# A two-layer graph network kernel: five PE transpositions per step become DMA transpositions of split rows

## The reference

```
# layer 0, x and adj of one graph; 8 heads of 32, 4 edge types
q, k = x @ Wq + bq, x @ Wk + bk
attn = softmax(q k^T / sqrt(32))                     # per head
out  = sum over r of (attn * (adj == r)) @ (x @ Wv[r] + bv[r])
x1   = LN(x + out @ Wo + bo) * g1 + beta1
x2   = LN(x1 + gelu(x1 @ W1 + b1) @ W2 + b2) * g2 + beta2
# layer 1, 8 heads of 32
e    = leaky(q k^T, 0.2), masked by adj > 0          # q, k, v = x2 @ Wq, Wk, Wv
h    = softmax(e) @ v
out  = LN(concat(LN(h) * g1 + b1, x2) @ Wffn^T) * g2 + b2 + x2
```

## Time and profile before

| | us |
|---|---|
| median of 3 runs | 2527.88 (2527.27 to 2528.18) |
| the profiled execution | 2530.18 |
| its span, first to last instruction | 2528.3 |
| PE busy | 2430.5 (96%) |
| ACT busy | 2212.6 (88%) |
| DVE busy | 2122.6 (84%) |
| POOL busy | 1925.9 (76%) |

### The profile page before, as it was taken

The page is one execution under the profiler, slowest core; times in us unless marked ns, Lnnn a source line. Parts: engine busy times, 40 slices in busy tenths (PEclk is TensorE's granted clock), DMA queues, the critical chain, the costliest instruction groups (busy, mean ns, idle before and its releaser), DMA issues. The chain is left out here.

```text
span 2528.3 us, 83141 instructions
## 1 busy us (share of the span) xinstructions
PE 2430.5 (96%) x31496; PEld 1984.4 (78%) x31496; DVE 2122.6 (84%) x3730; ACT 2212.6 (88%) x6224; POOL 1925.9 (76%) x2126
## 2 busy tenths in 40 slices
PE   3899999999999999999999999999999999999984
PEld 2678888888888888888888888878888888888873
DVE  3788888888889888889888888888888888888863
ACT  4699999989989989989989989989989989999973
POOL 1477787787788778778778778778778778778774
PEclk9999999999999999999999999999999999999997
DMA  5234433533433433443442442442443443443332
GB/s 135 58 55 83 93 61 80 93 67 75 93 71 71 93 75 67 93 78 63 94 82 59 94 83 59 93 87 59 88 92 57 85 94 60 81 93 61 77 64 47
DMA packets 610636, 196.75 MB, mean 78 GB/s; under 512 B 539328, under 2 KB 609472, under 8 KB 610240
## 3 DMA queue, kind: packets, MB, share of 16 engines
q1 hardware_dynamic: 607072, 188.02, 38.5%
q10 hardware_dynamic: 3168, 3.41, 0.5%
HBM read 40.38 MB, written 16.78 MB: 23 GB/s over the span
## 5 line engine op out<-in xcount | busy, mean ns | idle before, releaser
L982 DVE TENSOR_TENSOR pm<-pT,bank 128x4096 f16<-128x4096 f16 x256 | 567.6, 2279 | 0.0
L459 PE MATMUL bank<-wv,xT 128*128 128x512 f16 (+1 forms) x2304 | 456.6, 344 | 0.0
L1172 POOL TENSOR_TENSOR h<-h_f,h 128x512 f16<-128x512 f32 x256 | 297.3, 1174 | 117.5 <-ACT h L730 117.5
L459 PE MATMUL bank<-yT,w 128*128 128x256 f16 x3072 | 356.8, 273 | 1.2 <-DVE yT L944 1.2
L754 ACT ACTIVATE bank<-bank,p_nmax 128x128 f32<-128x128 f32 x1024 | 353.9, 364 | 4.4 <-DVE p_nmax L968 4.3
L459 PE MATMUL bank<-w,h 128*128 128x256 f16 x3072 | 347.3, 273 | 2.8 <-POOL h L1172 2.8
L459 PEld LDWEIGHTS bank<-wv,xT 128*128 128x128 f16 x2304 | 225.2, 98 | 148.3 <-issue 0.5
L743 ACT ACTIVATE p<-p,p_nmax 128x128 f32<-128x128 f32 x1024 | 336.0, 437 | 1.3 <-DVE p_nmax L961 0.6
L459 PEld LDWEIGHTS bank<-yT,w 128*128 128x128 f16 x3072 | 295.1, 98 | 42.8 <-issue 1.6
L459 PEld LDWEIGHTS bank<-w,h 128*128 128x128 f16 x3072 | 296.5, 98 | 37.4 <-issue 2.9
L1172 POOL TENSOR_TENSOR p1h<-p,p1h 128x512 f16<-128x512 f32 x256 | 296.6, 1159 | 30.5 <-ACT p1h L784 30.4
(11 more groups left out here) (127 smaller groups left out, 5663.7 us busy)
## 6 DMA issues: line engine op xcount, KB each, us to landing
x_sb<-in_x_dram SPq DMA_DIRECT2D x64, 256.0 KB, 3.4
adj_i<-in_adj_dram SPq DMA_DIRECT2D x128, 128.0 KB, 2.8
out_dram<-x2b SPq DMA_DIRECT2D x64, 256.0 KB, 2.3
pT<-p0h SPq DMA_TRANSPOSE x128, 4.9
pT<-p1h SPq DMA_TRANSPOSE x128, 4.7
pm<-in_L_gnn_W_dram ACTq DMA_DIRECT2D x1, 1024.0 KB, 13.6
pm<-in_L_gnn_W_dram SPq DMA_DIRECT2D x1, 1024.0 KB, 16.9
h_f<-in_L_gnn_Wffn_dram SPq DMA_DIRECT2D x1, 512.0 KB, 10.3
```

The source lines that it names most:

```text
L459: last = nc.tensor.matmul(o, l, r, start=(first and k == 0), stop=(k == len(todo) - 1))
L982: V_.tensor_tensor(pm0[g][:, s], pT0[g][:, s].unsqueeze(1).broadcast_to([P, REL, HEADS, P]), edges[:, g].unsqueeze(2).broadcast_to([P, REL ...
L1172: return V_.tensor_tensor(to, source, high, ALU.subtract)
```

## The change

- The five arrays are split into halves while still rows: ACT copies the high half into `x_rows`, `o0_rows`, `x1_rows`, `x2_rows`, `o1_rows` and POOL subtracts for the low half. SP then issues one `DMA_TRANSPOSE` of 256 KB for each (`transpose_rows`, line 427 of the new kernel), and PE waits for its landing. The twenty PE transposes of a pair are gone, and so are DVE's four low halves.
- The norm factor of `o1` is multiplied into the first half of Wffn in the preamble, and its shift becomes a row `w_bias`, added by one matmul of 512 columns per pair. `attention_affine_1` is gone.
- The norms of x1, x2 and the output run on DVE, in PSUM: one `scalar_tensor_tensor` subtracts the mean and multiplies by the factor row, a second multiplies by the root and adds the shift row (for the output, x2b). POOL's six large operations and two small ones, and ACT's `last_rows_normed`, are gone.
- x has three buffers and not two, and the bias bo is added in place. All lists of jobs are in another order, and so is `PE_BANKS`. The pipeline has 7 extra steps instead of 8.

```diff
+    ("f", 2, 3, "x2_ready", 1, 1),
+    ("v0_0", 1, 1, "v0_lo", 4, 1),
...
+                def transpose_x(m):
+                    sp.wait_ge(S["xT0_lo"], m + 1)
+                    if past(m):
+                        sp.wait_ge(S["v0_ps"], 4 * m)
+                        sp.wait_ge(S["q0_ps"], m)
+                        sp.wait_ge(S["k0_ps"], m)
+                    transpose_rows(xT0, x_rows, S["xT0_in"])
...
                 def x_transposed(m):
-                    pe.wait_ge(S["xT0_lo"], m + 1)
+                    pe.wait_ge(S["xT0_in"], 16 * m + 16)
...
                 def last_product(m):
                     u = m % 2
                     bank_free("w", m)
-                    pe.wait_ge(S["oT1_lo"], m + 1)
+                    pe.wait_ge(S["oT1_in"], 16 * m + 16)
                     x2_transposed(m)
+                    nc.tensor.matmul(ps("w")[:], ones16[:], w_bias[:].unsqueeze(1).broadcast_to([P, G, D]), start=True, stop=False)
...
                 def x1_high(m):
-                    act.wait_ge(S["yT0_ps"], m + 1)
-                    if past(m):
-                        act.wait_ge(S["h_ps"], 4 * m)
-                    nc.scalar.activation(flat(yT0[:, 0]), ps("yT0")[:], copy).then_inc(S["yT0_hi"], 1)
+                    act.wait_ge(S["x1_ready"], m + 1)
+                    if past(m):
+                        act.wait_ge(S["yT0_in"], 16 * m)
+                    nc.scalar.activation(x1_rows[:, 0], by_chunk(x1[:]), copy).then_inc(S["yT0_hi"], 1)
...
+                def centred_gained(name, gain, m):
+
+                    mv = ln[name][1]
+                    dve.wait_ge(S[name + "_mean"], 2 * m + 2)
+                    for g in range(G):
+                        last = V_.scalar_tensor_tensor(rows_in(name, g), rows_in(name, g), mv[:, g, 0:1], gain[:],
+                                                       ALU.subtract, ALU.mult)
+                    last.then_inc(S[name + "_gained"], 1)
+
+                def scaled_added(name, to, added, m):
+
+                    rs = ln[name][3]
+                    dve.wait_ge(S[name + "_gained"], m + 1)
                     dve.wait_ge(S[name + "_rstd"], m + 1)
                     for g in range(G):
-                        V_.tensor_scalar(rows_in(name, g), rows_in(name, g), mv[:, g, 0:1], rs[:, g:g + 1], ALU.subtract,
-                                         ALU.mult).then_inc(S[name + "_normed"], 1)
+                        last = V_.scalar_tensor_tensor(to[:, g], rows_in(name, g), rs[:, g:g + 1], added(g), ALU.mult, ALU.add)
+                    return last
...
+                def x1_low(m):
+                    pool.wait_ge(S["yT0_hi"], m + 1)
+                    low(x1_rows[:, 1], by_chunk(x1[:]), x1_rows[:, 0]).then_inc(S["yT0_lo"], 1)
```

More of the change, by code:

```diff
@@ L140, in build @@
         ident16 = sb("ident16", [P], BF16)
-        minus_half, minus_one = (sb(n, [G]) for n in ("minus_half", "minus_one"))
-        x_sb = [sb(f"x_sb{u}", [G, D]) for u in range(2)]
-        xbo = [sb(f"xbo{u}", [G, D]) for u in range(2)]
+        minus_half = sb("minus_half", [G])
+        w_bias = sb("w_bias", [D], F16)
+        x_sb = [sb(f"x_sb{u}", [G, D]) for u in range(XR)]
         adj0_i = sb("adj0_i", [G, P], I32)
@@ L327, in _ @@
                     last.then_inc(s_ffnT, 1)
+                pe.wait_ge(s_fold, 3 * KC)
+                for c in range(KC):
+                    last = nc.tensor.matmul(bank[2 * KC][:, 0:D], b1_cols[:, c], unscaled[:, c], start=(c == 0), stop=(c == KC - 1))
+                last.then_inc(s_ffnT, 1)
         S = {name: ctx.enter_context(nc.semaphore(name)) for names in SEMAPHORES.values() for name in names}
@@ L362, in pipeline, with landed @@
                 steps(n)
-        def landed(m):
-            return 16 * (m // 2) + 16
+        def landed(m, buffers):
+            return 16 * (m // buffers) + 16
         def flat(t):
@@ L453, in bank_free, with products @@
                         pe.wait_ge(*bank_before(job, m))
-                def products(o, pairs, first=True):
+                def products(o, pairs, first=True, final=True):
                     todo = [(l[i], r[j]) for l, r in pairs for i, j in ((0, 0), (0, 1), (1, 0))]
                     for k, (l, r) in enumerate(todo):
-                        last = nc.tensor.matmul(o, l, r, start=(first and k == 0), stop=(k == len(todo) - 1))
+                        last = nc.tensor.matmul(o, l, r, start=(first and k == 0), stop=(final and k == len(todo) - 1))
                     return last
@@ L829, in probs_high_0, with attention_high_1 @@
                                          copy).then_inc(S["p0_hi"], 1)
-                def last_rows_normed(m):
-                    act.wait_ge(S["w_shift"], m + 1)
+                def attention_high_1(m):
+                    act.wait_ge(S["o1_normed"], 2 * m + 2)
                     if past(m):
-                        act.wait_ge(S["out_ready"], m)
-                    for g in range(G):
-                        last = nc.scalar.activation(w_n[:, g], ps("w")[:, g * D:(g + 1) * D], ACT.Identity,
-                                                    scale=ln["w"][3][:, g:g + 1], bias=w_shift[:, g:g + 1])
-                    last.then_inc(S["w_normed"], 1)
@@ L1160, in _ @@
+                    if live(n):
+                        probs_low_0(n, 0)
                 pipeline(steps)
```

755 lines of the change are left out of this document (355 added, 400 removed).

## The result

The changed kernel takes 2407.75 us, the median of four runs (2403.04 to 2410.49); the kernel before, beside it, 2528.03. The ratio is 0.9519, 95% interval [0.9507, 0.9532]: 120 us less. The forecast was 2427, its own range 2415 to 2445, rival A (no stalls) 2409, and the range with 8 in 10 was 2400 to 2490. So the time lies in the wide range, outside the forecast's own, and on A's number. The profiled execution took 2403.04 us, with a span of 2401.2.

The account below looks back on a forecast made before the run. PE was taken as the bound, 37.67 us a step: span 2528.3 - 122.7 (PE work) + 17.7 (waits) + 4.0 (fill) = 2427.3, then + 1.9 - 2.3 = 2427 us. Own range 2415 to 2445; 8 in 10, 2400 to 2490.

Parts of the forecast that it names:

- rival A: PE in the steady steps: no stall at all, the forecast without its 17.7 us of waits, 2409 us; chance 0.22.
- PE's floor 35.59: PE's work in a step: 37.67 less 2.30 for the transposes plus 0.22 for the new matmul, 35.59 us.
- six take 1.30, one 0.22: The added w_bias matmul on PE: six matmuls of 512 columns take 1230.79 to 1232.09, so one costs 0.22 us.
- Waits 0.3 a step: PE's waits for the new transpositions to land: 0.3 us a step, 17.7 us in all.
- small spares: Landing before PE needs the array: x 0.3 us ahead, x2 0.1, x1 1.6.
- DVE 33.4, ACT 32.3, POOL 26.6: Work per step in us on the other engines after the change, all under PE's 35.59.
- 256 KB in 1.3 of issue and 3.3 to landing: Each small DMA transposition: half the issue of a 512 KB one, 1.3 us, plus 2.0 until it lands.
- Rival C: DMA transpositions cost by instruction, 256 KB as much as 512 KB: 2.9 us late per step, 2580 us; chance 0.08.
- Fill +4, drain 0: Ends of the run: fill 3.5 us longer for x's DMA plus 0.5 for folding the gain; drain unchanged, bounds -10 and +20.
- The executions: From span to median time: profiled execution 1.9 us over its span, median of the runs 2.3 under that execution.
- Rival B: The loop through x bounds, with DVE late to the last low halves: one more microsecond per step, 2480 us; chance 0.19.
- D: The new DVE operations cost 1.24 us each: DVE 43.5 us a step, 2876 us; chance 0.02.

Follow-up runs that it names:

- pe_back: The changed kernel with twenty fp32 transposes of the identity put back on PE per pair, result unused: 2532.34 us, ratio to the kernel before 1.0007.
- bias_split: The changed kernel with the four value-bias matmuls in two groups of two, the second after the values of the first graph: 2424.2 us, ratio 0.958.
- x_first: The changed kernel with the transpose of x issued before the first layer 0 probability transposition, into a second xT buffer: 2403.45 us, ratio 0.9497.
- extra_dma: The changed kernel with one more 256 KB DMA transposition per step, into an unread buffer, issued ahead of x's: 2457.66 us, ratio 0.971.
- before_x_dma: The kernel before with x alone, of the five arrays, split as rows and transposed by DMA: 2534.16 us, ratio 1.0022.
- before_x_dma_later: As before_x_dma, but ACT makes x's high half after the attention's high half: 2537.73 us, ratio 1.0034.

## Why the prediction was right, and where it was off

- **PE decides and a step falls by PE's work**: right for the changed kernel, and shown by pe_back. The price of the transposes (2.30 from the earlier trace rows) was 2.18 in that experiment.
- **PE's floor 35.59**: 0.39 too high. The step "six take 1.30, one 0.22" held. I took the biases as they stood and gave nothing for their order, though the order of PE's list ahead of the prediction already had the four in one run. bias_split gives 0.42 for it. This is the term of the sum that was mis-sized most: 0.39 in 59 steps is 23 us. Part of it went into waits again (next point), so the steady steps gave 121.1 us and not 105.0. These 16.1, 1.4 of the fill and 8.6 of the drain are the miss of 26.1 in the span.
- **Waits 0.3 a step**: 0.39, nearly right in size and half right in place. The small spares were real (x_first, extra_dma). Two waits were missed. The transpose of x2 waits for the last product of two pairs before, whose semaphore stands in SP's list; and the transposes of p1h, for which I laid out no times, are the largest of the three (11.3 of 22.4 us).
- **Rival A's number is luck**: A is the forecast without its 17.7 us of stalls, and the stalls came. 2407.75 is near its 2409 because the steady steps gave 16.1 us more than in the sum, fill and drain took 10.0 less, and the executions (below) put 7 back.
- **DVE 33.4, ACT 32.3, POOL 26.6**: 32.6 to 33.1, 32.8, 26.5. The new operation is 0.48 long, but two of them take 0.79 from start to start of the next (1214.00 to 1214.79 above), so 0.40 each is right. What I had wrong on DVE is o's normalising: two took 2.40 us and now take 1.15. I left it as it was, though it is long only while one of POOL's large operations runs, and the addition for x1b has moved away from beside it.
- **256 KB in 1.3 of issue and 3.3 to landing**: 1.24 and 3.2. Rival C, a cost by instruction, is out.
- **The rule on transposing DMAs** (the Trainium skill, "Advanced Engine Details and Errata", section "X-Bar Transpose (TRN2)"): 350 to 400 GB/s are not seen. The 1.24 us of issue are 211 GB/s for 256 KB, near the 212 of the earlier trace rows, and 2.40 for 512 KB are 218. (Issue times are read as rates here; the DMA engines' own pace shows in rows 6 alone.) extra_dma doesn't decide between 1.4 and 0.7 us on the DMA engines: with a spare of 0.3 they give 1.1 and 0.4 a step, and 0.8 was measured.
- **Fill +4, drain 0**: +2.6 and -8.6. The drain is the second term that was mis-sized. It may be that the passes of ACT and POOL in the last norm are worth more than the DMA in the last chains, or that it is the pipeline's 7 extra steps in place of 8, for which the prediction has no term. No run takes it apart.
- **The executions**: I put the median 2.3 us under the profiled run, as in the kernel before; here it is 4.7 above, in a spread of 7.5 us. Together with 1.8 for what lies around the span, where the prediction had 1.9, this takes back 7 of the 26 us, and the forecast is 19 too high.
- **Rival B** didn't come, because o's normalising, its main support, got faster and not slower. D is out by the 0.48.
- What I did not see is that taking work off PE was not enough. The prediction treats the change as five groups of transposes off PE, as if nothing lay close below. before_x_dma and before_x_dma_later show that one of the five, by itself, gives nothing, as a ring of 37.55 us lay under PE's 37.67. That the rest of the change opened this ring was not foreseen, and is the good luck in the right answer.

## What to carry to other kernels

An engine that is busy all of a step may have a ring of waits just below it: before work is taken off it, follow the resource that comes next (here a PSUM bank) once around the step and read its slack. In a queue that is served in order, a row that isn't ready holds up those behind it, so lay out the times of every row to the end of the queue and give the idle stretch to one that is ready. Small matmuls that each use 32 rows of the array (`tile_position` puts these four on different rows) are worth putting in one run, as four cost here what two do.

## What the runs showed of the hardware

- Four matmuls of 32 rows by 512 columns in one run took 0.32 us from start to start, as two did; split in two and two again the shortest step grew by 0.42 (bias_split).
- A DMA transposition of 256 KB, SBUF to SBUF, takes 1.24 us to issue and lands after 3.2 (3.0 to 5.6); one of 512 KB 2.4 and 4.6 (4.2 to 7.1).
- Two `scalar_tensor_tensor` on 128x256 fp32 took 0.88 us from PSUM beside a POOL subtraction of 512 columns, 0.88 from SBUF beside POOL operations of two columns only, and 1.84 from SBUF beside such a subtraction.
- A `tensor_scalar` on 128x256 fp32, SBUF to SBUF, took 0.40 us where POOL was idle. Where it began after a POOL operation on 512 columns it ended 0.15 us after that one, whatever its own length became: 0.83 us for o in the changed kernel, 1.13 and 1.35 for o before.
